# Graph attention on one core: TensorE's semaphore increments move from matmuls to drains of its queue

## The reference, cut to what matters

```python
e  = leaky_relu(concat(x[src], x[dst], ef) @ W_attn + b, 0.01)
m  = concat(x[src], ef) @ W_ne
ex = exp(e - segment_max(e, dst)[dst])
z  = segment_sum(ex / segment_sum(ex, dst)[dst] * m, dst)
out = layernorm(x + relu(concat(x, z) @ W_out))
```

## Time and profile before

| what | us |
| --- | --- |
| median of 3 runs (5343.77 to 5356.45) | 5353.08 |
| the profiled execution's own time | 5371.25 |
| its span, from the first to the last instruction | 5369.4 |
| PE busy | 2059.2 (38%) |
| DVE busy | 2577.0 (48%) |
| ACT busy | 2320.3 (43%) |
| POOL busy | 2978.2 (55%) |
| DMA engines, mean rate | 117 GB/s |
| mean granted clock of TensorE | 0.635 |

### The profile page before, as it was taken

How to read it: one execution, slowest core, us unless ns; L and a number is a source line. 1 busy time by engine, 2 the same in 40 slices (tenths; PEclk the granted TensorE clock), 3 DMA queues, 4 the chain that set the end, 5 groups by cost and what they waited for, 6 DMA issues and landing times.

```text
span 5369.4 us, 63828 instructions
## 1 busy us (share of the span) xinstructions
PE 2059.2 (38%) x9870; PEld 1946.1 (36%) x9871; DVE 2577.0 (48%) x4868; ACT 2320.3 (43%) x4121; POOL 2978.2 (55%) x3149
## 2 busy tenths in 40 slices
PE   1443443433333333333333334334333334333336
PEld 1343343433333333333333333333333333333336
DVE  5444444444444444444444445444445445444446
ACT  1444454444444444444444444444444444444444
POOL 5555555555555555555555555555555555555541
PEclk8666666666666666666666666666666666666666
DMA  5444444444444444444444444444444444444442
GB/s 111 128 118 118 120 119 127 120 117 119 118 115 122 118 109 123 118 119 122 119 114 111 118 118 122 114 119 129 107 118 127 109 118 129 118 118 120 120 118 56
DMA packets 759570, 628.92 MB, mean 117 GB/s; under 512 B 608412, under 2 KB 608796, under 8 KB 759332
## 3 DMA queue, kind: packets, MB, share of 16 engines
q1 hardware_dynamic: 646164, 519.51, 34.0%
q0 software_dynamic: 100096, 102.60, 9.8%
q10 hardware_dynamic: 13072, 4.80, 0.5%
HBM read 621.58 MB, written 4.81 MB: 117 GB/s over the span
## 4 chain that ended last, share of the span: by engine, by line
another core or an unknown queue 28%; issue 25%; ACT 16%; DVE 15%; DVEq 7%; ACTq 6%; PE 2%; POOL 0%
ACT psE L507 4%; ACT zb L508 4%; DVE prod L619 3%; DVE u L623 3%; ACT psS L499 3%; ACTq L513 2%; DVE e L689 2%; DVEq L741 2%; ACT acc L471 2%; DVE acc L682 2%; DVE um L728 1%; ACT nbias L497 1%; ACT ebias L502 1%; DVEq L708 1%
## 5 line engine op out<-in xcount | busy, mean ns | idle before, releaser
L365 POOL DMA_INDIRECT V<-in_x_dram,srcs x3128 | 2952.9, 944 | 2264.0 <-PEq L892 1328.7
L857 PE MATMUL psG<-V,pT 128*128 x6288 | 1456.6, 424 | 3078.6 <-DVE acc L682 2184.9
L857 PEld LDWEIGHTS psG<-V,pT 128*128 128x128 f32 x6288 | 1351.4, 326 | 3179.0 <-issue 3179.0
L461 ACT COPY pT<-psT 128x512 f32<-128x512 f32 x784 | 428.8, 582 | 1800.6 <-remote 1593.3
L689 DVE TENSOR_TENSOR e<-zb,psE 128x1024 f32<-128x1024 f32 x392 | 477.2, 1217 | 1269.6 <-remote 1240.7
L619 DVE TENSOR_TENSOR prod<-V,psM 128x1024 f32<-128x1024 f32 x391 | 477.6, 1221 | 497.8 <-issue 497.7
L728 DVE CUSTOM_DVE_ANT_0 um<-ubc,psS 128x1024 f32<-128x1024 f32 x391 | 476.1, 1218 | 356.4 <-ACT psS L499 256.2
L851 PE MATMUL psT<-ident,e 128*128 128x128 f32 x3136 | 586.5, 350 | 0.0
L851 PEld LDWEIGHTS psT<-ident,e 128*128 128x128 f32 x3136 | 558.1, 214 | 0.0
L623 DVE TENSOR_REDUCE u<-prod 128x8 f32<-128x1024 f32 x391 | 477.1, 1220 | 48.0 <-issue 12.9
L508 ACT ACTIVATE zb<-um,ebias 128x1024 f32<-128x1024 f32 x391 | 443.1, 1133 | 0.0
(11 more groups left out here) (95 smaller groups left out, 497.5 us busy)
## 6 DMA issues: line engine op xcount, KB each, us to landing
ubc<-scores SPq DMA_DIRECT2D x391, 512.0 KB
dbc<-in_dst_dram SPq DMA_DIRECT2D x390, 512.0 KB
V<-in_edge_attr_dram SPq DMA_DIRECT2D x390, 256.0 KB
V<-in_x_dram,srcs POOLq DMA_INDIRECT x3128
scores<-u SPq DMA_DIRECT2D x391, 4.0 KB
srcs<-in_src_dram SPq DMA_DIRECT2D x390, 4.0 KB
out_dram<-y SPq DMA_DIRECT2D x12, 256.0 KB
xt<-in_x_dram ACTq DMA_DIRECT2D x6, 448.0 KB
```

The lines of the kernel that those rows point to most:

```text
L365: nc.gpsimd.indirect_dma_start(V[0:n, s, j, 0:F], None, x[:, :], bass.IndirectOffsetOnAxis(ap=srcs[0:n, s, j:j + 1], axis=0)).then_inc(h_i ...
L461: nc.scalar.copy(pT[:, i, :], psT[:, i, :]).then_inc(pt[i], 1)
L857: last = nc.tensor.matmul(psG[:, 0:AW], pT[:, i, j * P:(j + 1) * P], V[:, bass.ds(sv, 1), 4 * i + j, :].rearrange("p a f -> p (a f)"), sta ...
```

## The change

Inside the loop no matmul carries an increment any more. The two halves of products are followed by two drains that carry `agg_half` and `agg_done`, and the eight transposes by two drains that carry `tr[0]` and `tr[1]`. PE no longer waits for `agg_done` before it frees a slot: a drain carries the increment of `v_free`. The product for a pair of node blocks is followed by a drain with `y_ready`. The last of these products, outside the loops (L904), keeps its own increment.

```diff
@@ y_pair
-                y_multiply().then_inc(y_ready, 1)
+                y_multiply()
+                pe.drain().then_inc(y_ready, 1)
@@ turn(i)
                 for j in range(4):
-                    last = nc.tensor.transpose(...)
-                last.then_inc(tr[i], 1)
+                    nc.tensor.transpose(...)
@@ multiply(i, sv)
                 for j in range(4):
-                    last = nc.tensor.matmul(...)
-                last.then_inc((agg_half, agg_done)[i], 1)
+                    nc.tensor.matmul(...)
@@ window
                 multiply(1, sv)
+                pe.drain().then_inc(agg_half, 1)
+                pe.drain().then_inc(agg_done, 1)
                 if turns:
                     pe.wait_ge(mx_done, G)
                     turn(0)
                     turn(1)
+                    pe.drain().then_inc(tr[0], 1)
+                    pe.drain().then_inc(tr[1], 1)
@@ supertile
                     pe.load(coming, trip[0:1, bass.ds(2 * t + 3, 1)])
-                    pe.wait_ge(agg_done, pe.snap(g))
-                    pe.sem_inc(v_free[(s - BEHIND) % RING], 1)
+                    pe.drain().then_inc(v_free[(s - BEHIND) % RING], 1)
```

More of the change, by code:

```diff
@@ L850, in turn @@
                 for j in range(4):
-                    last = nc.tensor.transpose(psT[:, i, j * P:(j + 1) * P], e1[:, :].rearrange("q (p j) -> q j p", j=J)[:, 4 * i + j, :], ident[:, :])
-                last.then_inc(tr[i], 1)
+                    nc.tensor.transpose(psT[:, i, j * P:(j + 1) * P], e1[:, :].rearrange("q (p j) -> q j p", j=J)[:, 4 * i + j, :], ident[:, :])
             def multiply(i, sv):
                 for j in range(4):
-                    last = nc.tensor.matmul(psG[:, 0:AW], pT[:, i, j * P:(j + 1) * P],
-                                            V[:, bass.ds(sv, 1), 4 * i + j, :].rearrange("p a f -> p (a f)"),
-                                            start=(i == 0 and j == 0), stop=(i == 1 and j == 3))
-                last.then_inc((agg_half, agg_done)[i], 1)
+                    nc.tensor.matmul(psG[:, 0:AW], pT[:, i, j * P:(j + 1) * P],
+                                     V[:, bass.ds(sv, 1), 4 * i + j, :].rearrange("p a f -> p (a f)"),
+                                     start=(i == 0 and j == 0), stop=(i == 1 and j == 3))
             def window(turns):
```

## The result

| kernel | median us | runs | lowest to highest |
| --- | --- | --- | --- |
| before | 5354.76 | 6 | 5343.77 to 5381.56 |
| after | 5386.80 | 6 | 5382.55 to 5390.19 |

The ratio is 1.0054, with a 95% interval of 1.0028 to 1.0079: 0.5% slower, where 19% faster was forecast. The profiled execution took 5387.09 us and its span 5384.5. The time lies outside the range and is on the other side.

A forecast was written before the change was run, and what follows sets the result against it. Late matmul increments beside gathers were taken as the bound, gathers as the next. 115.3 + 390 x 10.62 + 88.7 + 5 drains + 1.9 made 4352.7, scaled by 0.9966 to 4338 us, 19% less; range 4090 to 5200 us.

The forecast's parts named there:

- Increments leave the matmuls: TensorE's loop: drains carry the increments instead, removing their lateness beside gathers if a drain ends when the array is done.
- the 4.6 us a window: Loop interval between weighings: 13.245 us against 8.65 without gathers, the difference lost to something that goes with the gathers.
- it is the increment that is late: TensorE's matmuls beside gathers: the report comes late, 1.7 to 16 us behind the transposes, not the array's work.
- late while gathers run, and on time when none does: Increments carried by matmuls: 1.7, 9 and 16 us late in windows beside gathers, not late after the last gather.
- The first rival: Drains behind the transposes end only when late increments would have come; stalls remain, 0.78 us a window added, 5658 us; chance 0.15.
- The slot is freed behind the transposes: `v_free` comes up to 1.9 us later than behind the products; costs nothing, as slots are in stock.
- Five drains a window: TensorE's queue: about 0.05 us each beyond the work awaited; four between products and copies, 0.2 us (0 to 1.1).
- The first copy 0.8 us later, `y_ready`, `agg_*`: Copies after turning: 0.8 us a window, hidden by gathers except 5 us after the last; the other increments cost nothing.
- What is late next is GpSimd: Eight gathers bound each window from below at 9.97 us; with one slow window in four, 10.62 us.
- The lower sum: Whole kernel with 9.97 us for each interval: 4099.2 us, or 4085 as the median of runs.
- Sequencers' slowness: Rival: beside continuous gathers other engines' sequencers become the bound, most windows 12.33 us, 5003 us; chance 0.24.

The follow-up runs named there:

- held job: Set of runs on one chip where the kernel before took 5354.76, 5180.69 or 5342.76 us; TensorE's completions come late beside gathers.
- free job: Set of runs on one chip where the kernel before took 4025.75 or 4024.74 us; TensorE's completions are on time beside gathers.
- job A: Held runs: single parts of the change against the kernel before (5180.69 us), and the kernel after with gathers or loads cut; the kernel after itself absent.
- e3: Kernel before with drains behind the transposes only, carrying tr[0] and tr[1], and one with y_ready: 5122.06 us, ratio 0.9906.
- job D: Free runs: kernel before 4024.74 us, kernel after 4025.69, kernel before with only the slot's drain 4025.29, kernel after with six or four gathers 3725.06 and 3732.05.
- job C: Free runs: kernel before 4025.75 us, kernel after 4024.73, kernel before with only the slot's drain 4026.21, and that with GpSimd pauses 6885.59 and 4941.03.

## Why the prediction was wrong

*"Increments leave the matmuls. This removes the lateness if a drain ends when the array is done."* This is the step that failed. In a held job a drain is late as a matmul's increment is: the drains behind the transposes took 5.57 us at the median, for work of 1.95 us at most. In a free job neither is late, and a window takes 9.9 us. So the lateness goes with the state and not with who carries the increment; of the 4.6 us a window, a free job gives back 3.3 (13.2 against 9.9), and there GpSimd's gathers are the bound. My two grounds for "it is the increment that is late" were both weak. The halves released at one moment fit a hold that lets everything go at its end, and the window of the earlier trace rows has them 7.1 us apart. And the increment of 51 ns is the duration of an instruction that asks nothing of the array. The sentence that "no row shows a drain inside the loop" was the honest one, and the chance should have followed it. The step before it, "late while gathers run, and on time when none does", was off as well. Of the gathers beside the earlier trace rows the last is

```profile
2716.18 0.95 POOL L365 DMA_INDIRECT V<-in_x_dram,srcs  x1 [0.30 <-issue]
```

It ends at 2717.13, before the transposes do (2717.44), and still their increments come 1.7 us late, 2.0 us behind that gather. The tail of a hold stood in the trace of before. The Trainium skill's page "Perfetto Trace Analysis", section "Tensor Engine Instruction (MATMUL, LD_WEIGHTS)", stood against the step, and the traces agree with the reading of it that I made a rival: whatever is late for the matmul's update is late for the drain, at 5.57 us in place of 1.95.

*The first rival, "the drain waits for what is late",* is what happened. Its point of decision, a drain over 1.7 us behind the transposes, was passed in more than half of the windows (the median of L876 is 3.6 us above 1.95). Its price, 5658 us, was 271 us too high: it kept the stalls of the earlier trace rows as they were, and they went.

*"The slot is freed behind the transposes ... nothing."* This is the term that brought the stalls down. In job A it is worth 222 us (5180.69 - 4958.83). Freed behind the products, a slot can come while a run still goes on, and the run goes on to 16 gathers: before, 73 of 74 runs of 16 have such an increment (L892) within them, and 157 of 160 runs of eight have none. And 73 of the 74 lie beside a window over 20 us, as in the earlier trace rows. Freed behind the transposes, the next run mostly starts when the hold is over: 255 runs of eight in the kernel after, and 62 of 15 or 16 against 96 before. Runs of 16 alone don't make the long windows, though: e3 has 80 of them and two intervals over 20 us.

*Five drains a window, 0.2 us.* Undisturbed, a copy starts 0.05 us behind the transposes' end (job D), so a drain costs no more than I took from the earlier trace rows. I priced only what a drain adds behind its work, not what queues behind it. Held, the one behind the products keeps the transposes back (ratio 1.05 alone), and the ones behind the transposes keep the load of the next count and `v_free` back by 1.0 us a window (1.80 against 0.81 us from copy to gather). That these two eat the 4% of the slot's drain is likely, not shown: the ratios of single parts are from job A, where the kernel after did not run. By the reckoning put down for job C they make 1.04 on 5181 us, some 5390; elsewhere the kernel after took 5386.80 and 5379.42, at a ratio of 1.005 and 1.0065 to a slower kernel before.

*The first copy 0.8 us later, `y_ready`, `agg_*`:* hidden, as forecast, in a free job, where none of it shows. The drain with `y_ready` took 63.6 us in its 49 cases, with the work it waits for; what it costs in a held job was not tested alone.

*"What is late next is GpSimd", 9.97 to 10.62 us a window.* Right as a bound in a free job and wrong as an effect: in job D a window takes 9.905 us at the mean in the kernel after, and before has the same time to 0.02%. That the sum comes near is no merit of the change. The lower sum, 4085 us, is 1.5% above the 4025.69 measured. It describes what any of these kernels does where nothing is held.

*Sequencers' slowness.* It goes with the held state too. Beside the first 80 gathers VectorE came round in 38.1 us in the kernel after's first profile (L718 to L718, 65.63 to 103.71; the earlier trace rows has the like before). In job D, the same kernel beside the same gathers, it took 8.63:

```profile
61.47 0.34 DVE L718 TENSOR_SCALAR wnode<-node,half 128x3 f32 x1 [2.07 <-issue]
...
70.10 0.45 DVE L718 TENSOR_SCALAR wnode<-node,half 128x3 f32 x1 [0.90 <-DVE u L623]
```

The first trace of the kernel after has 1372 register, branch and semaphore instructions of VectorE, ScalarE and SP that took 680 to 760 ns; that of job D has none.

What stays open: what the held state is, and whether the work in the array or only the report of its end is delayed. Other work on GpSimd in a held job (a plain DMA on its own queue, or plain writes), and the kernel after with its load moved ahead of the turn's drains, were not run. Of the versions run, the fastest in a held job is the kernel before with the one edit of `v_free` (0.9594); in a free job it ties. It ran beside the kernel after only in free jobs, so that it is 8% faster than that in a held one rests on two jobs (4958.83 against 5386.80 and 5379.42).

## What to carry to other kernels

If completions are late, first find out when they come, against every other engine's activity, before changing who reports them: here the last gather of a run, 2 us ahead of the late increments, was in the trace of before. Moving an increment from an instruction to a drain moves it behind everything in the queue and moves the queue behind it; price both. Where a resource is handed back decides in which rhythm the other engine works: that one edit gained 4% in a held job, and no drain put in for a matmul's increment gained as much.

## What the hardware showed that was not expected

- The same program took 5355, 5181 or 5343 us in three jobs and 4026 and 4025 us in two, with spreads inside a job of 0.1 to 1.5%. A ratio near one can hide a state in which the kernel has another bound.
- In the held state TensorE's completions are on time up to some 5 us into a run of indirect gathers of GpSimd. Later ones mostly come behind the last gather of the run: 1.1 us behind it for four gathers, 1.4 for six, 1.7 for eight, 3.1 to 3.5 for 15 or 16. Some come in mid-run: in all 80 runs of 16 of e3, a drain ended some 7 us into the run. The hold is there with 16 rows in a gather as with 128. With a plain DMA of SP for the same bytes and no gather it was not seen (one run, its state not certain).
- A write of 0.97 us and a drain on GpSimd's queue, once before every eight gathers, cost 2.34 us each time (one run, in a free job).
